# A language adapter and a conditional linear layer: x transposed on VectorE from a second load, the up projection in float32, beta added later

## What is computed

```python
h       = relu(x @ W1[lang] + b1[lang])              # 512 -> 128, the up projection
adapted = h @ W2[lang] + b2[lang]                    # 128 -> 512, the down projection
y       = x + adapted
normed  = (y - mean(y)) * rsqrt(var(y) + 1e-5)       # over the 512 features
x1      = x + normed * gamma[lang] + beta[lang]
out     = x1 + x1 @ W[cat] + b[cat]                  # 512 -> 512, the linear layer
```

## Time and profile before

| | |
|---|---|
| median of 3 runs | 688.96 us (687.92 to 689.35) |
| span of the profiled execution | 683.6 us |
| TensorE, VectorE busy | 667.4 us (98%), 545.6 us (80%) |
| ScalarE, GpSimd busy | 505.0 us (74%), 446.6 us (65%) |
| granted TensorE clock, mean | 0.995 |
| DMA | 134.55 MB, 57.9% of 16 engines' span |

### The profile page before, as it was taken

The page is one execution under the profiler, slowest core; times in us unless marked ns, Lnnn a source line. Parts: engine busy times, 40 slices in busy tenths (PEclk is TensorE's granted clock), DMA queues, the critical chain, the costliest instruction groups (busy, mean ns, idle before and its releaser), DMA issues.

```text
span 683.6 us, 12284 instructions
## 1 busy us (share of the span) xinstructions
PE 667.4 (98%) x3425; PEld 551.5 (81%) x3425; DVE 545.6 (80%) x1129; ACT 505.0 (74%) x992; POOL 446.6 (65%) x359
## 2 busy tenths in 40 slices
PE   8789999999999999999999999999999999999997
PEld 7668887888888888888888888888878888888885
DVE  2788888888888878888888887888888888887873
ACT  4777778877778787778787778877778887777850
POOL 4746776666776666876666777666777666777640
PEclk9999999999999999999999999999999999999999
DMA  7453665556665556666565675645675655675522
GB/s 239 164 187 122 218 200 217 186 181 229 215 217 206 189 174 228 215 224 206 187 205 192 215 245 186 215 175 192 215 246 188 206 207 174 221 233 191 182 88 94
DMA packets 67239, 134.55 MB, mean 197 GB/s; under 512 B 8770, under 2 KB 26268, under 8 KB 63260
## 3 DMA queue, kind: packets, MB, share of 16 engines
q1 hardware_dynamic: 67228, 134.43, 57.9%
HBM read 100.71 MB, written 33.55 MB: 196 GB/s over the span
## 4 chain that ended last, share of the span: by engine, by line
PE 78%; DVE 9%; ACT 6%; issue 4%; DMA 1%; SPq 1%; DVEq 0%
PE o_bank L668 14%; PE o_bank L669 14%; PE o_bank L670 14%; PE n_bank L706 8%; PE x_bank L695 7%; PE d_bank L668 6%; PE d_bank L670 5%; PE d_bank L669 5%; ACT norm L424 5%; DVE y L527 2%; DVE xT_lo L512 1%; DVE neg_mean L531 1%; PE x_bank L668 1%; PE x_bank L669 1%; PE x_bank L670 1%
## 5 line engine op out<-in xcount | busy, mean ns | idle before, releaser
L338 POOL TENSOR_TENSOR x_tok<-x_tok,b_bc 128x512 f32<-128x512 f32 x128 | 161.7, 1296 | 116.8 <-PE x_bank L695 116.8
L668 PE MATMUL o_bank<-w_hi,x1T_hi 128*128 128x512 f32 x512 | 209.2, 409 | 1.9 <-DVE x1T_lo L573 1.5
L670 PE MATMUL o_bank<-w_hi,x1T_lo 128*128 128x512 f32 x512 | 201.6, 394 | 0.0
L669 PE MATMUL o_bank<-w_lo,x1T_hi 128*128 128x512 f32 x512 | 200.4, 391 | 0.0
L344 POOL TENSOR_TENSOR w_lo<-w_raw,w_hi 128x512 fp32r<-128x512 f32 x128 | 163.0, 1307 | 9.4 <-ACT w_hi L403 9.4
L424 ACT ACTIVATE norm<-y,neg_mean 128x512 f32<-128x512 f32 x128 | 91.0, 713 | 67.8 <-DVE neg_mean L531 67.8
L670 PEld LDWEIGHTS o_bank<-w_hi,x1T_lo 128*128 128x128 f32 x512 | 96.3, 188 | 21.8
L668 PEld LDWEIGHTS o_bank<-w_hi,x1T_hi 128*128 128x128 f32 x512 | 96.7, 189 | 19.8 <-issue 1.8
L669 PEld LDWEIGHTS o_bank<-w_lo,x1T_hi 128*128 128x128 f32 x512 | 97.0, 189 | 18.2
L567 DVE SCALAR_TENSOR_TENSOR n_bank<-n_bank,params,xT_beta 128x512 f32<-128x512 f32 x126 | 91.9, 752 | 24.0 <-PE n_bank L706 24.0
L407 ACT ACTIVATE x1T_hi<-n_bank 128x512 fp32r<-128x512 f32 x126 | 75.6, 600 | 45.5 <-DVE n_bank L567 43.6
(11 more groups left out here) (80 smaller groups left out, 994.4 us busy)
## 6 DMA issues: line engine op xcount, KB each, us to landing
w_raw<-in_L_cond_W SPq DMA_DIRECT2D x32, 1024.0 KB, 5.3
out<-out_half SPq DMA_DIRECT2D x63, 512.0 KB, 3.0
x_tok<-in_x SPq DMA_DIRECT2D x31, 1024.0 KB, 4.9
w_raw<-in_L_cond_W SPq DMA_DIRECT2D x64, 256.0 KB, 5.4
b_bc<-in_L_cond_b SPq DMA_DIRECT2D x64, 256.0 KB, 6.6
x_tok<-in_x SPq DMA_DIRECT2D x2, 512.0 KB, 3.8
params<-param_table SPq DMA_DIRECT2D x32, 4.5 KB, 1.7
out<-out_half SPq DMA_DIRECT2D x2, 256.0 KB, 2.4
```

Source lines behind the costliest of these rows:

```text
L338: pool.tensor_tensor(x_tok[p][:, t, :], x_tok[p][:, t, :], b2_bc[p][:, :], ALU.add).then_inc(x_b2_done, 1)
L668: pe.matmul(acc, lhs_hi, rhs_hi, start=first, stop=False)
L669: pe.matmul(acc, lhs_hi, rhs_lo, start=False, stop=False)
L670: return pe.matmul(acc, lhs_lo, rhs_hi, start=False, stop=last)
```

## The change

x comes a second time, in four DMAs of a feature quarter each: feature q * 128 + c * 32 + i of token b * 32 + j goes to partition q * 32 + j of `x_quad`, at block b, column c * 32 + i. VectorE's 32x32 block transpose of chunk c then gives `xT` with feature q * 128 + c * 32 + i on partition q * 32 + i and the 512 tokens along the row. So the feature chunks are taken in another order everywhere: W1, W and the parameter table are loaded by quarters, and `normalise` writes the norm in that order. The tokens of x and out lie as (t p) in place of (p t), so their rows in DRAM are 2 KB pieces.

The transposes of x on TensorE, xT_hi, xT_lo, x plus beta, and the high and low parts of W1 are gone. The up projection is four float32 matmuls on `w1_raw` and `xT`. x1 in the bank is without beta; `high_x1` and `low_x1` add it.

```diff
+            def load_x_quads(s, p):
+                for n in range(NQ):
+                    sp.dma_start(x_quad[p][quad(n), :, :],
+                                 x_quads[bass.ds(s, 1), n].rearrange("o j b f -> j (o b) f")
+                                 ).then_inc(xq_in[p], 16)
...
             def load_w(g, p):
-                sp.dma_start(w_raw[p][:, :, :], w_rows[bass.ds(g, 1)].rearrange("o p c h -> p (o c) h")
-                             ).then_inc(w_in[p], 16)
+                for n in range(NQ):
+                    sp.dma_start(w_raw[p][quad(n), :, :],
+                                 w_rows[bass.ds(g, 1), n].rearrange("o i c h -> i (o c) h")
+                                 ).then_inc(w_in[p], 16)
...
-                    load_x(k.sample(-1), q)
-                    load_w12(lang, q)
+                    load_x_quads(k.sample(-1), q)
+                    load_w12(lang, q)
+                    load_x(k.sample(-1), q)
                     load_b2(lang, q)
...
                     if k.since(1):
-                        sp.wait_ge(x1_done, k.count(NC, 0, 0))
+                        sp.wait_ge(x1_lo_done, k.count(NC, 0, 0))
                     load_params(lang, q)
...
-                    pool.wait_ge(w_in[q], 16 * k.pairs(1) + 16)
-                    raw = w_raw[q][:, :, :]
-                    blocks = bass.AP(raw.tensor, raw.offset, [[NC * H, P], [H + P, NC], [1, P]])
-                    pool.tensor_tensor(blocks, blocks,
-                                       ident[:, :].rearrange("p (o n) -> p o n", o=1).to_broadcast([P, NC, P]),
-                                       ALU.add).then_inc(diag_done, 1)
+                    pool.wait_ge(w_in[q], 16 * NQ * k.pairs(1) + 16 * NQ)
+                    for c in range(NC):
+                        block = chunk_columns(w_raw[q][:, c, :], c)
+                        pool.tensor_tensor(block, block, ident[:, :].rearrange("p (q i) -> p q i", q=NQ),
+                                           ALU.add).then_inc(diag_done, 1)
...
-                    pool.wait_ge(xT_done, k.count(NC, 0, NC))
+                    pool.wait_ge(x_in[p], 16 * k.pairs(0) + 16)
...
-                act.wait_ge(diag_done, k.count(1, 0, 0))
                 for c in range(NC):
+                    act.wait_ge(diag_done, k.count(NC, 1, c + 1))
                     act.activation(w_hi[q][:, c, :], w_raw[q][:, c, :], ACT.Copy).then_inc(w_hi_done, 1)
...
-                act.activation(x1T_hi[1 - k.p][:, c, :], norm_bank(k, c)[:, :], ACT.Copy).then_inc(x1_hi_done, 1)
+                act.activation(x1T_hi[q][:, c, :], norm_bank(k, c)[:, :], ACT.Identity,
+                               bias=params[q][:, NC + c:NC + c + 1]).then_inc(x1_hi_done, 1)
...
+            def turn_x(k, c):
+
+                if c == 0:
+                    dve.wait_ge(xq_in[k.p], 16 * NQ * k.pairs(0) + 16 * NQ)
+                dve.transpose(xT[k.p][:, c, :].rearrange("p (b j) -> p b j", j=SQ),
+                              x_quad[k.p][:, :, c * SQ:(c + 1) * SQ]).then_inc(xT_done, 1)
...
-                dve.tensor_tensor(x1T_lo[q][:, c, :], norm_bank(k, c)[:, :], x1T_hi[q][:, c, :].bitcast(F32),
-                                  ALU.subtract).then_inc(x1_lo_done, 1)
+                dve.scalar_tensor_tensor(x1T_lo[q][:, c, :], norm_bank(k, c)[:, :],
+                                         params[q][:, NC + c:NC + c + 1], x1T_hi[q][:, c, :].bitcast(F32),
+                                         ALU.add, ALU.subtract).then_inc(x1_lo_done, 1)
...
                 for c in range(NC):
-                    ins = split_product(d_bank[0][:, :], w1_hi[k.p][:, c, :], w1_lo[k.p][:, c, :],
-                                        xT_hi[:, c, :], xT_lo[:, c, :], c == 0, c == NC - 1)
+                    pe.wait_ge(xT_done, k.count(NC, 0, c + 1))
+                    ins = pe.matmul(d_bank[0][:, :], w1_raw[k.p][:, c, :], xT[k.p][:, c, :],
+                                    start=c == 0, stop=c == NC - 1)
```

More of the change, by code:

```diff
@@ L58, in adapter_then_conditional_linear, with quad, chunk_columns, by_chunk @@
     assert A == P and NT == 4 and NC == 4 and S % 2 == 0
[L61 to L64, removed]
+    NQ, SQ = 4, 32
+    NB = T // SQ
+    x_rows = x.rearrange("s (t p) h -> s p t h", p=P)
+    x_quads = x.rearrange("s (b j) (q f) -> s q j b f", j=SQ, q=NQ)
+    out_rows = out.rearrange("s (t p) h -> s p t h", p=P)
+    w1_rows = W1.rearrange("l (q c i) a -> l q i c a", q=NQ, c=NC)
+    w_rows = W.rearrange("g (q c i) o -> g q i c o", q=NQ, c=NC)
+    def quad(n):
+        return slice(n * SQ, (n + 1) * SQ)
+    def chunk_columns(row, c):
+        return row.rearrange("p (q c i) -> p q c i", q=NQ, c=NC)[:, :, c, :]
+    def by_chunk(row):
+        return row.rearrange("p (c q i) -> p q c i", q=NQ, c=NC)
+    def by_quad(row):
+        return row.rearrange("p (q c i) -> p q c i", q=NQ, c=NC)
     ctx = ExitStack()
@@ L84, in adapter_then_conditional_linear @@
         params = [sb(f"params{i}", [P, NP]) for i in range(2)]
[L86 to L90, removed]
+        x_quad = [sb(f"x_quad{i}", [P, NB, NC * SQ]) for i in range(2)]
+        xT = [sb(f"xT{i}", [P, NC, T]) for i in range(2)]
         w2_hi = [sb(f"w2_hi{i}", [P, H], F32R) for i in range(2)]
@@ L144, in adapter_then_conditional_linear @@
         rows_in = sem("rows_in")
-        x0_left_in = sem("x0_left_in")
+        xq_in = [sem(f"xq_in{i}") for i in range(2)]
         x_in = [sem(f"x_in{i}") for i in range(2)]
@@ L268, in step @@
                     store(k, 2, 1)
-            left, right = slice(0, H // 2), slice(H // 2, H)
-            sp.dma_start(x_tok[0][:, :, left], x_rows[0, :, :, left]).then_inc(x0_left_in, 16)
             sp.dma_start(ids[0:1, 0, :], lang_ids.rearrange("(o s) -> o s", o=1)).then_inc(lang_in, 16)
-            for rows, at in ((gamma, 0), (beta, L * NC)):
-                sp.dma_start(param_rows[at:at + L * NC, :], rows.rearrange("l (c p) -> (l c) p", p=P)
-                             ).then_inc(rows_in, 16)
-            sp.dma_start(param_rows[2 * L * NC:L * NP, :], b1).then_inc(rows_in, 16)
-            sp.dma_start(x_tok[0][:, :, right], x_rows[0, :, :, right]).then_inc(x_in[0], 16)
-            sp.dma_start(ids[0:1, 1, :], cat_ids.rearrange("(o s) -> o s", o=1)).then_inc(cat_in, 16)
+            load_x_quads(0, 0)
             sp.wait_ge(lang_in, 16)
@@ L448, in step @@
                 if follow:
-                    high_w12_of_next(k)
+                    high_w2_of_next(k)
                 if adapter:
                     deviation(k)
+            for c in range(NC):
+                for rows, at in ((gamma, c * P), (beta, H + c * P)):
+                    act.dma_start(param_rows[:, at:at + P].rearrange("l (q i) -> l q i", q=NQ),
+                                  chunk_columns(rows, c)).then_inc(rows_in, 16)
+            act.dma_start(param_rows[:, 2 * H:2 * H + A], b1).then_inc(rows_in, 16)
             act.wait_ge(ident_done, 2)
@@ L557, in normalise @@
             def normalise(k, t):
[L560 removed]
+                dve.tensor_scalar(by_chunk(norm[:, t, :]), by_quad(y[:, t, :]), rstd[:, t:t + 1], neg_mean_rstd[:, t:t + 1],
                                   ALU.mult, ALU.add).then_inc(norm_dve_done, 1)
```

195 lines of the change are left out of this document (59 added, 136 removed).

## The result

| | before | changed |
|---|---|---|
| median | 689.15 us (687.92 to 689.98, 4 runs) | 760.57 us (759.00 to 762.05, 4 runs) |
| span of the profiled execution | 683.6 us | 759.6 us |
| granted TensorE clock, mean | 0.995 | 0.96 |
| one step | 20.40 us | 22.72 us |

A forecast was written before the change was run, and what follows sets the result against it. The prediction took a ring through W's load as the bound: 19.85 + 2.6 = 22.45 us a step against 20.40, 30 x 2.05 = +61 us; 683.6 + 61 + 5.4 = 750 us, range 655 to 775.

The forecast's parts named there:

- ring: Step-to-step loop over W's load, GpSimd, ScalarE, TensorE and VectorE: 19.3 us, 19.85 with neg_mean held, 22.45 with slower landing.
- three waits: New in each step: ScalarE's w_hi for the diagonal, the diagonal for w_raw's DMA, SP's params for x1T_lo.
- TensorE's 19.0 us: TensorE's work in one changed step: 60 x 0.23 + 1.76 + 3.5 us; alone, 42 us would go.
- float32 changes nothing while the ring binds: Up projection on TensorE: float32 at 1.8 or 3.5 us makes no difference to the time while the ring binds.
- 21.0 were added up: DMA volume in a step at the slow end: 12.4 us plus x 5.3, W 2.6, w1 0.7, of 22.45.
- rival 3: DMA queue saturates: 512-byte pieces of x at 100 GB/s cost 10.5 us; step 26 us, 857 us; chance 0.04.
- Two: ... I take 2.6: Landing of W in four DMAs onto 32 partitions: 0 to 2.6 us more than today, 2.6 taken.
- It holds the first neg_mean ..., 0.76 long: VectorE, within the 5.07 us from start of down to low_x1(3): first neg_mean lasts 0.76 us, as today.
- the second neg_mean: VectorE: comes 12.2 us after the start of GpSimd's 13.1 us run, inside w2_lo; held 0.56 us.
- 730 - 170 ns: Size of the hold on a small VectorE operation beside GpSimd: var_eps median less minimum, 0.56 us taken.
- Head and tail I put at zero: Outside the loop: head loses TensorE's transposes but waits for x, each some 2 us; tail stays; zero net.
- the 5.4 us between span and median: Median of the kernel before, 688.96 us, above its profiled span of 683.6; added to the forecast.

The follow-up runs named there:

- run 1: Changed kernel with the load of W moved ahead of SP's wait for x1_lo_done and of params: 674.53 us, ratio 0.9825 to the kernel before.
- run 4: Changed kernel with W loaded ahead of params and GpSimd's diagonal, x plus b2 and w2_lo held behind rstd, VectorE's norm and both neg_mean: 647.75 us, ratio 0.9423.
- run 2: Changed kernel with one wait added: GpSimd makes the low part of W2 only after both neg_mean. 721.53 us, ratio 1.049.
- run 3: Changed kernel with W in one DMA onto 128 partitions, leaving out the chunk order of W's rows: 733.40 us, ratio 1.0662.
- Run 8: Kernel before with params waiting for x1_lo_done, and GpSimd's low parts of W1 and W2 waiting for both neg_mean: 681.89 us, ratio 0.9942.
- Run 12: Changed kernel with only the first two of the four float32 up matmuls, leaving out half the features there: 757.30 us, ratio 1.1043.
- run 5: Kernel before with the changed wait alone, params waiting for x1_lo_done in place of x1_done: 749.78 us, ratio 1.0915.
- run 6: Kernel before with W loaded by four DMAs of 32 partitions alone, same rows in the same places: 700.62 us, ratio 1.0208.

## Why the prediction was right, and where its terms were off

**Right, and shown.** A ring from W's issue to the next W's issue is the bound: three waits were named and are there, runs 1 and 4 open the ring, and runs 2 and 3 shorten it by 1.3 and 0.9 us, with the time following. Run 8 takes away the whole loss of the moved wait in the kernel before. TensorE's 19.0 us is what appears once it is open (18.88 in run 4). Run 12 bears out that float32 changes nothing while the ring binds. The DMAs take 80.7% of the span, 19.2 us in a step, where 21.0 were added up; rival 3's 100 GB/s for the quarters of x stood in no row, and its step of 26 us did not come. Up matmuls: 8 records in 3.60 us, 3.5 taken. Block transposes: 0.687, 0.65 taken. w_hi, high_x1 with low_x1, norm transposes with linear tile 2, and issue: 2.10, 2.11, 3.31, 0.91 against 2.2, 2.05, 3.2, 0.8.

**Two terms were wrong, with opposite signs, and with one of them a stretch of the path.** "Two: ... I take 2.6" for the landing of W: it is 6.63 in place of 8.1, so 1.1 more than in the kernel before. The rate is 0.6 of W's before (244 against 404 GB/s), where the sum took half; and the first quarter is moving while the others are still being issued. And "It holds the first neg_mean ..., 0.76 long": kept as before, it is 2.67. I had moved the second neg_mean into GpSimd's run (0.56) and let the first stand, though GpSimd's run starts after W in the new ring and so shifts against VectorE's order; the second is free (0.17). The errors of the landing and of the holds are 1.5 too much and 1.9 - 0.56 = 1.3 too little.

The prediction had the numbers for this. By its own terms the first neg_mean comes 7.9 + 2.3 = 10.2 us after the start of a GpSimd run of 13.1, so it would be held for 2.9. That makes the ring 19.3 - 0.76 + 2.9 = 21.4, and with its own 2.6 for the landing 24.0, or 797 us, outside the range. With the measured 1.1 it is 22.5. So that 22.45 came so near to 22.72 is in part luck. And what the hold means is that GpSimd's run, and not the chain over w_hi, `high_x1` and the norm transposes, leads from GpSimd's start to neg_mean; those terms were sized rightly, but with 2.5 us to spare they did not set the step.

**The size of the hold.** The 730 - 170 ns were taken from a single GpSimd instruction in the way. In run 5 and in the changed kernel an operation was held over one or two of GpSimd's instruction boundaries to the end of the run, in most steps.

**The landing of W.** By the figures of the Trainium skill (SBUF — State Buffer, Door 1: The DMA port swizzle), 189 against 328 GB/s, the prediction had an estimate of 2.3 us later. The ratio of the rates agrees, 0.58 there and 243 against 404 GB/s, 0.60, in run 6; the estimate for one 1 MiB transfer does not carry over to four that start one behind another. The quarters came 1.1 us later in run 6 (1.3 in the median over the steps), and 0.8 between run 3 and the changed kernel.

**Head, clock, offset.** "Head and tail I put at zero": the rest, some 6 of the 76.0 us, is in the head, where r of the first sample comes at 28.9 in place of 23.3 us. The clock was left out. After a hole in TensorE's work the clock is at its lower level, 1.2 of 2.4 GHz, here for 3.25 us at least (stretch, us, TensorE busy, clock, DMA share, GB/s):

```profile
341.50:343.75 2.25, 0.19 (x1) 1.00 0.00 0
344.50:347.75 3.25, 3.25 (x10) 0.50 0.87 210
```

That costs TensorE, not the ring, which runs past it over GpSimd, VectorE, SP and the DMA. And the 5.4 us between span and median belong in part to the one execution shown: where both are on record, a run's time is 1.8 to 2.0 us above its own span, so the profiled execution of the kernel before was some 3.5 us shorter than the median. In the changed kernel the median is 1.0 above the span.

**Where the 71 us come from.** The kernel before with the moved wait: +63. Quarters on top: +24 (alone, without the moved wait: +14, so the split depends on the order). The rest of the change, float32, block transposes and fewer copies: about -15, by the ratios, 1.1257 to 1.1038; without the quarters, run 5 against run 3, about -17. In that pair GpSimd's run to the end of neg_mean is 13.84 and 12.96 us, which is the 0.9 us by which the steps differ: GpSimd has lost the low part of W1, and TensorE's gain has no share in it. What the change's own work is worth once the ring is open, run 4 shows; its price was a wait and a layout beside it.

**Open.** Why neg_mean is let in between two GpSimd instructions in some steps (0.39 at 354.25) and not in others (2.93 at 398.37), from starts that lie alike, no run tells.

## What to carry to other kernels

When a buffer is to be read longer, look at what stands behind its reload in the queue, and put the large load ahead of the wait: it was worth some 83 us here. When a load comes later, ask which engine's run it starts, and what of VectorE that run then covers; a slack before the next reader (5.5 us in the kernel before) says nothing of it. When times around a ring add up to the step, that is no proof that each of them counts: look which chain ends last at each point where two meet. And a wait added at the right place can be the cheapest gain: one line took 67 us from run 5.

## What the runs showed of the hardware

- Small VectorE operations that meet GpSimd's run last until an instruction of it ends, or until the run ends: 1.04, 1.43, 2.67 and 2.93 us in place of 0.17. `y`, 512 columns with one input in a bank, takes 0.65 to 0.69 us in every step of every kernel here, and `r`, with one input, its 0.13 to 0.18. The Trainium skill (SBUF — State Buffer, Who interferes with whom) states that tensor_scalar in a faster mode, and operations with two SBUF inputs, shut out GpSimd and are shut out by it, whoever starts first, for the whole instruction. Which operations are held agrees with that; 2.93 us is longer than any one instruction of GpSimd in that run (1.34).
- Four DMAs onto 32 partitions each move 243 or 244 GB/s in the mean (run 6, changed kernel) with all engines busy; one onto 128 partitions, 404. From issue to use that is 6.7 us for 1 MiB, against 5.4 to 6.0 with one DMA, by the medians of the runs.
- Four DMAs onto 128 partitions whose source has an outer dimension of four: about 100 GB/s, a quarter of the engines, and issues of 1.4 us.
- Float32 matmuls of 512 columns: two records each, 0.45 us apart (3.60 us for eight). The block transpose of 128x512 float32 on VectorE: 0.687 us.
